# A three-branch graph, attention and expert kernel: 13 row chunks cut anew, turned rows kept in device memory, graph messages moved to VectorE

## What is computed

```
xn  = layernorm(x)
gnn = sum over 4 heads of alpha[n, h] * (xn @ W)[dst[n], head h]       # 64 wide, repeated 4 times; alpha: softmax over heads
q, k, v = split(xn @ w_qkv + b);  k, v = layernorm over each head's 32
kv  = k^T v / N   (8 heads, 32 x 32);   ret = q @ kv + xn
mix = gelu(ret @ w1 + b1) @ w2 + b2 + xn
x2  = x + gnn + mix
y   = sum over 8 experts e of  w[n, e] * (relu(bn(relu(bn(z W1[e])) W2[e])) Wo[e] + bo[e]),   z = layernorm(x2)
out = x2 + y
```

## Time and profile before

| | |
|---|---|
| median of 3 runs | 1177.97 us (1177.38 to 1178.65) |
| the profiled execution, its own time | 1180.07 us |
| its span, first to last instruction | 1178.2 us |
| PE busy | 1121.4 us (95%) |
| DVE / ACT / POOL busy | 819.6 (70%) / 734.6 (62%) / 354.3 us (30%) |
| moved by DMA | 42.1 MB |

### The profile page before, as it was taken

One profiled execution on the slowest core, in us unless ns is written; L12 is line 12 of the kernel. 1 busy time (PEld: TensorE's weight loads), 2 busy tenths in 40 slices (PEclk: granted clock), 3 DMA queues, 4 the chain that ended last, 5 costly groups with the idle time before them and its releaser, 6 DMA issues. The chain is left out here.

```text
span 1178.2 us, 19388 instructions
## 1 busy us (share of the span) xinstructions
PE 1121.4 (95%) x6714; PEld 993.8 (84%) x6714; DVE 819.6 (70%) x1798; ACT 734.6 (62%) x1244; POOL 354.3 (30%) x306
## 2 busy tenths in 40 slices
PE   5899984699999999999999999999999999999998
PEld 3788873589888888888888988988888888888887
DVE  6889873486775865867758667586586775865553
ACT  3677751375666666666666566665666656656665
POOL 2667665351060330601504205033060150400100
PEclk9899995799999999999999999999999999999999
DMA  4455433000100100101001010010010100100000
GB/s 117 126 129 154 122 85 74 19 11 10 37 20 1 37 19 20 37 1 38 19 1 46 10 37 19 1 37 19 10 46 1 37 19 1 25 2 19 1 1 22
DMA packets 60661, 42.12 MB, mean 36 GB/s; under 512 B 26262, under 2 KB 58746, under 8 KB 60564
## 3 DMA queue, kind: packets, MB, share of 16 engines
q1 hardware_dynamic: 56452, 34.28, 11.0%
q0 software_dynamic: 4112, 6.61, 2.2%
HBM read 27.86 MB, written 13.00 MB: 35 GB/s over the span
## 5 line engine op out<-in xcount | busy, mean ns | idle before, releaser
L1092 DVE SCALAR_TENSOR_TENSOR accumulated<-bank,router_w,accumulated 128x256 f32<-128x256 f32 (+1 forms) x392 | 169.9, 479 | 200.0 <-PE bank L228 169.1
L477 ACT ACTIVATE h<-weight_stage 128x512 fp32r<-128x512 f32 (+1 forms) x208 | 114.8, 599 | 211.6 <-PE bank L228 206.9
L226 PE MATMUL bank<-ffn_w_high,h 128*128 128x256 f32 (+1 forms) x784 | 221.8, 283 | 1.0 <-DVE h L910 1.0
L228 PE MATMUL bank<-ffn_w_high,h 128*128 128x256 f32 (+1 forms) x784 | 221.8, 283 | 0.0
L227 PE MATMUL bank<-ffn_w_low,h 128*128 128x256 f32 (+1 forms) x784 | 221.8, 283 | 0.0
L910 DVE TENSOR_TENSOR h_low<-activated,h_high 128x512 fp32r<-128x512 f32 (+1 forms) x210 | 156.4, 756 | 67.5 <-ACT h_high L477 66.7
L584 ACT ACTIVATE weight_stage<-bank,bn_cols 128x512 f32<-128x512 f32 (+1 forms) x208 | 156.8, 754 | 57.0 <-PE bank L228 56.1
L584 ACT ACTIVATE activated<-bank,bn_cols 128x512 f32<-128x512 f32 (+1 forms) x208 | 157.1, 755 | 50.3 <-PE bank L228 48.4
L449 POOL TENSOR_TENSOR residual<-residual,b_rows 128x1024 f32<-128x1024 f32 (+1 forms) x13 | 29.6, 2273 | 515.9 <-DVE residual L1112 515.9
L226 PE MATMUL bank<-xT_high,ffn_w_high 128*128 128x512 f32 (+1 forms) x416 | 162.8, 391 | 0.0
L226 PE MATMUL bank<-h_high,ffn_w_high 128*128 128x512 f32 (+1 forms) x416 | 159.5, 383 | 0.0
(11 more groups left out here) (183 smaller groups left out, 2075.6 us busy)
## 6 DMA issues: line engine op xcount, KB each, us to landing
x_rows<-in_x SPq DMA_DIRECT2D x20, 512.0 KB, 5.0
node_table<-gathered SPq DMA_DIRECT2D x48, 130.0 KB, 2.9
out<-accumulated SPq DMA_DIRECT2D x12, 512.0 KB, 3.3
weight_stage<-in_L_ffn_W SPq DMA_DIRECT2D x16, 256.0 KB, 4.2
accumulated<-in_x SPq DMA_DIRECT2D x4, 512.0 KB, 5.0
weight_stage<-in_L_ffn_Wo SPq DMA_DIRECT2D x8, 256.0 KB, 4.2
gathered<-node_table,indices POOLq DMA_INDIRECT x49
alpha_l<-node_alpha_l,indices POOLq DMA_INDIRECT x49
```

The costliest lines, as they stand in the source:

```text
L226: nc.tensor.matmul(dst, ah, bh, start=(k == 0 and not lead), stop=False)
L228: last = nc.tensor.matmul(dst, al, bh, start=False, stop=(k == n - 1))
L477: return nc.scalar.activation(dst, src, ACT.Copy)
L1092: last = V.scalar_tensor_tensor(a, Yb[b][0:tp, (t % 2) * D:(t % 2 + 1) * D], wts(ch)[0:tp, t, e:e + 1], a, ALU.mult, ALU.add)
```

## The change

1. **Chunks.** `ROWS = [252] + 11 * [512] + [366]`, 13 chunks as before. A chunk's tile has rows / tiles rows: the first chunk two tiles of 126, the last three of 122, all others four of 128; 49 tiles as before. `Chunk` and `Tile` carry first row, first tile (`g0`) and first bank pair (`b0`), and all waits count by these.
2. **Turned rows.** The first pass stores each pair of tiles of `xTh` and `xTl` to a new tensor `x_turned`; the second pass loads `xmh`, `xml` from it. The transposes of `xn`, their two splits, and DVE's write of `xn` go. `base` is formed by one DVE instruction with the row bias b2 in it. `t_hi` and `t_lo` now wait for stores.
3. **Messages** go from POOL to DVE: per tile and head one instruction 64 wide, then one add of 256. POOL keeps the gathers (now behind the square root of its chunk and behind `gmsg`) and the square root.
4. **kv matrix** in six wide DVE steps; its copies shared between ACT and DVE; w1 is added in PE's accumulation; the last tile's k and v are summed by PE.
5. **Chores** later: batch-norm at tiles 8 to 15, others before or behind their old places; statistics of x chunk 1 ahead of the first weights; statistics of x chunk 2 from tile 0 on; index loads for chunk 0 early; `xt_evict` moved behind `xnormed` in ACT's order; PE waits for the last weight split only before the first expert. In the first chunk the messages stand behind `gel_split`.

The core of the diff:

```diff
-NFULL = N // CH
-TAIL = N - NFULL * CH
+ROWS = [252] + 11 * [CH] + [366]
+NC = len(ROWS)
@@ SP
+            def store_turned(pair):
+                cols, ch = pair_cols(pair), pair[0].ch
+                need(sp, s["tlo"], pair[-1].g + 1)
+                for i, part in enumerate((xTh, xTl)):
+                    sp.dma_start(xt_d[ch.c, i, :, :, cols], part[:, ch.par, :, cols].bitcast(fp32)).then_inc(s_xst[ch.par], 16)
+            def load_turned(ch):
+                need(sp, s["fm2"], ch.b0)
+                need(sp, s_xst[ch.par], turned_stored(ch))
+                for i, part in enumerate((xmh, xml)):
+                    sp.dma_start(part[:, :, 0:ch.rows].bitcast(fp32), xt_d[ch.c, i, :, :, 0:ch.rows]).then_inc(s["xm"], 16)
+            store_turned(TILES[0:2])
+            load_idx(CHUNKS[0])
             for i in range(NTILES + LAG):
+                if i >= 1 and pair_ahead(i - 1):
+                    store_turned(pair_ahead(i - 1))
                 if i + 3 in JOB_AT:
                     load_job(JOB_AT[i + 3])
+                if i in LOAD_AT:
+                    need(sp, s["xnorm"], CHUNKS[LOAD_AT[i].c - 2].g0)
+                    load_x(LOAD_AT[i])
+                if i == NTILES - 2:
+                    load_turned(CHUNKS[0])
+                    need(sp, s["xnorm"], NTILES)
+                    load_rows(CHUNKS[0])
+                    load_rows(CHUNKS[1])
+                ... node_table and alpha_l stores as before, rows of the tile
+            load_turned(CHUNKS[1])
+            load_idx(CHUNKS[1])
+            for ch in CHUNKS:
+                if ch.c > 0:
+                    store(ch.prev())
+                if ch.c + 2 < NC:
+                    load_rows(CHUNKS[ch.c + 2])
+                    load_idx(CHUNKS[ch.c + 2])
+                    load_turned(CHUNKS[ch.c + 2])
@@ POOL
+            gather(CHUNKS[0])
+            for ch in CHUNKS:
+                norm2(ch)
+                if not ch.last:
+                    need(pool, s["gmsg"], ch.c + 1)
+                    gather(ch.next())
@@ PE
-            def turned(ch, src):
+            def mix1(ch):
+                need(pe, s["fai"], ch.b0)
+                need(pe, s["xm"], 32 * (ch.c + 1))
+            FRONT = {2: mix1, 3: mix2, 5: x2_turn, 6: router}
@@ DVE, the middle
+            md.step(V.tensor_scalar(t1, Sb[:, 0:2 * P], gvc[:, :], None, ALU.mult))
+            dve.wait_ge(s["m_sum"], 1)
+            md.step(V.scalar_tensor_tensor(t1, Tb[:, 0, :], bvc[:, :], t1, ALU.mult, ALU.add))
+            V.scalar_tensor_tensor(kvq[:, :], Tb[:, 1, 0:2], gvc[:, :], bvn[:, :].broadcast_to([P, 2]), ALU.mult, ALU.add)
+            V.tensor_tensor(t1g, t1g, gk2.unsqueeze(1).broadcast_to([P, 2, P]), ALU.mult)
+            for grp in range(2):
+                V.scalar_tensor_tensor(kvT[:, grp, :], bk2, kvq[:, grp:grp + 1], t1g[:, grp, :], ALU.mult, ALU.add)
@@ DVE, second pass
+            def messages(ch):
+                ... sum, reciprocal, alpha
+                for h in range(GH):
+                    for t in range(nt):
+                        if h == 0:
+                            last = V.tensor_scalar(m, src, al, nmA[...], ALU.mult, ALU.add)
+                        else:
+                            last = V.scalar_tensor_tensor(m, src, al, m, ALU.mult, ALU.add)
+                    sm.step(last)
+                for t in range(nt):
+                    last = V.tensor_tensor(b, b, Gt[0:tp, t, 0:GC].unsqueeze(1).broadcast_to([tp, GH, GC]), ALU.add)
+                last.then_inc(s["gmsg"], 1)
+            FRONT = {0: (base_rows, logits), 1: (messages,), 2: (gel_split,), 3: (x2,), 4: (x2_norm,), 5: (x2_low,), 6: (route,)}
+            for step in (base_rows, logits, gel_split, messages, x2, x2_norm, x2_low, route, weights):
+                step(CHUNKS[0])
```

More of the change, by code:

```diff
@@ L45, in rows_of, with pairs, __init__ @@
     def rows_of(self, dram):
-        part = dram[self.c * CH:self.c * CH + self.rows, :]
+        part = dram[self.row0:self.row0 + self.rows, :]
         return part.rearrange("(t p) d -> p t d", p=self.tp)
+    def pairs(self):
+        return [range(2 * b, min(2 * b + 2, self.nt)) for b in range(self.nb)]
 class Tile:
[L53 to L56, removed]
+    def __init__(self, ch, t):
+        self.ch, self.t, self.tp = ch, t, ch.tp
+        self.g = ch.g0 + t
+        self.slot = self.g % TPC
+        self.row = ch.row0 + t * ch.tp
 def need(eng, sem, value):
@@ L191, in build @@
         s_wst = [s["wst0"], s["wst1"], s["wst2"]]
+        s_xst = [s["xst0"], s["xst1"]]
         s_tab = [s["tab0"], s["tab1"]]
         s_out = [s["out0"], s["out1"]]
[L195 to L198, removed]
         accx = acc[:, 0, :, :]
@@ new lines, in router_turn, with out_bias @@
+            def router_turn(ch):
+                tp = ch.tp
+                need(pe, s["fw3"], ch.c + 1)
+                for t in range(ch.nt):
+                    last = nc.tensor.transpose(Fb[1][:, t * P:t * P + tp], w3[0:tp, t, :], ident[0:tp, 0:tp])
+                last.then_inc(s["fw3T"], 1)
+            def out_bias(ch):
+                tp = ch.tp
+                need(pe, s["fw3c"], ch.c + 1)
+                for b, pair in enumerate(ch.pairs()):
+                    for t in pair:
+                        last = nc.tensor.matmul(Fb[b][0:tp, (t % 2) * D:(t % 2 + 1) * D], w3T[:, t, 0:tp], bo3[:, :],
+                                                start=True, stop=True)
+                    last.then_inc(s["fbo"], 1)
@@ L892, in chunk_b @@
                     if e == 0:
[L893 to L897 removed]
+                        out_bias(ch)
+                    if nxt is not None and e in FRONT:
+                        FRONT[e](nxt)
             L3(LAST, NE - 1)
@@ L1200, in _ @@
-            smalls = {(0, False): 3, (1, False): 2, (2, False): 0, (3, False): 1, (4, False): 0, (5, False): 0,
-                      (6, False): 3, (6, True): 4, (7, True): 0}
-            OFF, PER = {}, 0
-            for key in smalls:
-                OFF[key] = PER
-                PER += smalls[key]
-            for e in range(NE - 1):
-                front(chunk(0), e)
-            front(chunk(0), NE - 2, end=True)
-            hid1(chunk(0), 0)
-            def chunk_b(ch):
+            smalls = {"logits": 3, "messages": 7, "x2": 1, "route": 3, "weights": 4}
@@ L1223, in chunk_b @@
                     if nxt is not None and e == NE - 1:
-                        front(nxt, NE - 2, end=True)
+                        weights(nxt)
                     hid2(ch, e)
                     if e == 0:
-                        front(ch, NE - 1, end=True)
-                    if nxt is not None and e < NE - 1:
-                        front(nxt, e)
-            for ch in CHUNKS:
-                chunk_b(ch)
+                        add_bias(ch)
+                    if nxt is not None:
+                        for step in FRONT.get(e, ()):
+                            step(nxt)
             accumulate(LAST, NE - 1)
```

790 lines of the change are left out of this document (398 added, 392 removed).

## The result

The changed kernel took 1176.57 us (median of 20 runs, 1173.91 to 1178.57), the kernel before 1178.06 beside it: ratio 0.9985, 95% interval 0.9979 to 0.9992. That is 1.5 us where 10 were forecast, and within the 0.2% that I called no change. The profiled execution has a span of 1173.8 us against 1178.2.

The account below looks back on a forecast made before the run. PE, busy 95% overall and without a gap from 240 to 1100 us, was taken as the bound. The sum 1178.2 - 16.4 + 5 - 18.3 + 13 + 6.7 gave 1168.2, forecast 1168 us, range 1148 to 1184.

Parts of the forecast that it names:

- Part 1: Expert loop from 240 us on: new cut and removed transposes (0.79 us per full chunk) give -16.4 us, DVE's messages covered.
- Part 2: Chunk 0's short expert steps cannot cover the next front, and chunk 1's gathers come late: +5 us, bounds 0 and +12.
- The third rival: Chunk 0 starves and the loop does not keep its gain: +9 us, 1177 us, chance 0.17.
- Part 3: Middle, up to the first expert matmul: gathers start at 188, first expert matmul at 207.9 us, -18.3 us.
- the wide kv steps: Middle: six wide DVE steps worth nothing by themselves, hidden by the graph side with some 7 us to spare.
- Part 4: First pass: turned stores, the larger last x load and a later start cost +13 us.
- The start: First pass, tiles 0 and 1 delayed by chunk 2's statistics, and ten DMAs before the first table store: +4 (-2 to +8).
- The traffic of turned stores: First pass: 12.8 MB of added stores fit the queue but lengthen waits for stores: +5 us (0 to +25).
- The x load of 366 rows: First pass: last chunk's x load holds two engines for 9.6 us, with table stores behind it: +4 us.
- Part 5: End: last output store grows from 106 to 366 rows at 39 GB/s, +6.7 us; at full rate -1.6.
- the first rival: 122-row transfers run at the full rate, gaining in middle, first pass and end: 1148 us, chance 0.18.
- The second rival: First pass becomes bound by the store round, `xt_evict` waiting for stores: 1179 to 1195 us, chance 0.20.

Follow-up runs that it names:

- e5: The changed kernel run once more, not edited: 1184.2 us, ratio 1.0053 against the kernel before.
- e9: e8 with the turned rows of chunk 0 and x rows of chunks 0 and 1 issued behind the last table stores: 1147.6 us.
- e4: The changed kernel with x of chunk 2 loaded ahead of the 27 small loads: 1175.1 us.
- e3: The changed kernel without the stores of turned rows for chunks 3 to 12, output not the reference's: 1177.1 us.
- e11: The changed kernel with the old chunks, 12 x 512 and 106 rows: 1181.1 us.
- e14: e7 with chunk 2's four alpha gathers held back until PE has done chunk 1's first layer, its table gathers left in place: 1151.4 us.
- e1: The changed kernel with chunks of 240 and 378 rows in place of 252 and 366: 1167.8 us.
- e7: e1 with x of chunk 2 also loaded ahead of the 27 small loads: 1159.4 us.
- e8: e7 with the gathers of chunk 2 also held back until PE has done chunk 1's first layer: 1153.1 us.
- e2: The changed kernel with only the last output store split in two DMAs, of 112 and 10 partitions: 1178.1 us.

## Why the prediction was wrong in its size

**Part 1, the loop: right.** 0.89 us per full chunk for 0.79, and the loop without chunk 0's stall came to -15.4 for -11.4, since chunk 0 lost little in that profile. **Part 2, chunk 0:** the mechanism that I priced (fronts too big for short steps, messages on DVE) is there and small: gaps of 0.4 to 0.6 us ended by `h_low` and `mix_xT_low`, 0.9 us in all in the quick profile and 1.6 in `e5`, inside the bounds of 0 to 12. The gathers of chunk 1 waited 3.5 us for their indices (2 forecast) and so ran beside the first experts. The mechanism that matters, matmul issue stalling beside the gathers of chunks 1 and 2 and the clock behind it, 8.5 us between the two profiles of one program, I did not name. It is not what the profile of the result lost, but it is why the same kernel also runs at 1184. The third rival (chunk 0 starves) gave 1177, and the median came out at 1176.6; that is luck, as in that profile the loop kept all that it was given. For the runs at 1184 its place, chunk 0, was right, but not its cause.

**Part 3, the middle:** -16.7 for -18.3. The gathers started 22.7 us after tile 48; I had 188 - 167 = 21; from there to the first expert it took 19.8 us for 19.9. That the wide kv steps are hidden by the graph side held, with 15 us between their end and the gathers. What I did not see is that SP issues `load_turned` and both `load_rows`, 1.3 MB (not the 1.5 that I wrote for `e9`), ahead of the last stores: `e9` puts 3.5 us of the middle on it.

**Part 4, the first pass, is the step that failed: +21.1 for +13.** Its terms, mis-sized one by one:
- The start, 4 allowed (up to 8), was 8.5 (`e4`). I knew that the statistics of chunk 2 now stand ahead of tile 0's sums and that x landed at 26.8, but took the delay as the 3.85 us that were waited before, not as the distance from where DVE now arrives, 16.75 us. Before, DVE had other steps until 22.9; with the chores moved it has none.
- The traffic of turned stores, 5 allowed, was 6.8 (`e3`), and the landing of a turned half was 3.7 to 4.4 us. A table store waits behind two of them.
- The x load of 366 rows, 4 allowed: the one wait was 6.1 us; the cut to 378 took 7.5 us off the first pass, and going back to 12 x 512 and 106 rows 4.6 (`e11`).

The three add up to 19.9 or 22.8, by the last term, against 21.1 found. Each was measured by taking it away alone, and they may overlap.

A part of the miss is no step of the kernel: the sum was made on a span that stood 0.2 us from the median, but only because that execution took 2 us more than the median. The changed kernel's median lies 2.8 us above its profiled span, so of the 8.4 us between 1168.2 and 1176.6 the parts account for 5.6 (+8.1, +1.6, -4.0 and -0.1).

**Part 5, the end: right,** +6.6 for +6.7; and the first rival, that 122-row transfers run at the full rate, is out: 39 GB/s for 122 rows, and -7.2 us once the same rows are sent as 112 and 10 partitions. The Trainium skill ("DMA: Bandwidth & Descriptors", Why a DMA increments its semaphore by 16 and not by 1) gives two engines to 122 partitions, sixteen to 112 and ten to 10. The trace agrees: DMA share 0.11 is two of 16, and the split store was through in under 2 us. **The second rival** was right in part: the waits of `xt_evict` for stores did grow, from 13.0 to 30.4 us, and 6.8 us of that reached the end. It wanted +23 us and more in the first pass; that this came to +21.1, just short of it, owes 8.5 us to the start, which the rival does not name.

Since gains and losses of 32 and 28 us nearly cancel, 8 us of error in one term turned a clear gain into none. The range, 1148 to 1184, held the time; the chance of 0.12 for no change was too low for a sum that small beside its terms.

## What to carry to other kernels

When a step moves ahead in an engine's order, price its wait from when the engine now gets there to when the data land, not from the wait that was there before. Choose odd chunk sizes by the partitions of their tiles: one line, 240 and 378 for 252 and 366, took 16 us off the slow case and 9 off the quick one. And when three edits each win in their place and nothing at the end, look for what their profiles share behind it, and run the base once more.

## What the runs showed of the hardware beyond that

- A row of eight indirect DMAs in 10 us beside nine short matmuls a microsecond (240 to 256 columns) stalled the issue of matmuls at the end of the row: PE idle for 1.6 us in 6 beside the gathers of chunk 1 and 2.1 us in 4 beside those of chunk 2 (`e5`), and at neither place in the quick profile of the same program. ACT lost time at the same place (1.24 us busy from 236 to 239 us in `e5`, 2.94 in the quick profile, in both from 5.4 us into the loop on). Beside six matmuls a microsecond eight gathers did not do it, nor did the four table gathers of `e14`. What couples them no row shows.
- Behind the 2.1 us of idle time in `e5`, in gaps of at most 0.8 us, the granted clock went from 1.00 to 0.50 (2.4 to 1.2 GHz) for 3 us, from 279 to 282; in `e1` it stayed there for 10 (262 to 272). Behind the 1.6 us of the first stall it stayed at 1.00. Idle time and clock together put the loop of `e5` back by 4.7 us at the second stall; in `e7` against `e8` it was 6.6.
- A store split by partitions in 112 + 10 went at 218 to 341 GB/s in the full slices of its profile (`e2`), against 39 for the same 122 partitions in one DMA.
